# Six load slots for three, and the shift grids cleared by GpSimd, in a four-stage convolution and attention kernel

## The reference

```python
x = x + _L0_conv_ref(_gn(x), ...)   # shifted-window attention, 8 heads, windows of 8x8 at stride 2, then a projection
x = x + _L1_conv_ref(_gn(x), ...)   # grouped 3x3 convolution (32 groups), batch norm over all pixels, relu
x = x + _L2_conv_ref(_gn(x), ...)   # 1x1, 3x3 and 1x1 convolutions, each scanned over channel blocks, A + x
x = x + _L3_conv_ref(_gn(x), ...)   # the same with other weights
```

## Time and profile before

| | us |
|---|---|
| median of three runs | 2324.82 (2323.87 to 2324.83) |
| the profiled execution | 2317.36 |
| its span, first to last instruction | 2315.6 |
| first transpose to last statistics of the load | 5.2 to 75.7 |
| start of the tail stage | 1278.4 |
| first product of the strips | 1320.3 |

### The profile page before, as it was taken

One profiled execution on the slowest core, in us unless ns is written; L12 is line 12 of the kernel. 1 busy time (PEld: TensorE's weight loads), 2 busy tenths in 40 slices (PEclk: granted clock), 3 DMA queues, 4 the chain that ended last, 5 costly groups with the idle time before them and its releaser, 6 DMA issues. The chain is left out here.

```text
span 2315.6 us, 72190 instructions
## 1 busy us (share of the span) xinstructions
PE 2016.2 (87%) x29330; PEld 1068.7 (46%) x29330; DVE 1700.2 (73%) x3482; ACT 1150.2 (50%) x2577; POOL 1060.1 (46%) x1228
## 2 busy tenths in 40 slices
PE   5699889997999799986999279888999999999996
PEld 5455555554555455543566023333444433333332
DVE  5698999899888989893333788887776665566653
ACT  5576666765666566662223345444443433333330
POOL 0477777776777677765910364332222211111100
PEclk9899999999999999997999599999999999999997
DMA  7211101111111011101444777775444443444444
GB/s 269 85 37 37 49 34 36 50 36 47 36 50 36 33 50 36 51 33 57 103 102 104 273 268 228 212 238 160 128 130 141 139 119 101 122 123 125 123 102 110
DMA packets 225593, 243.72 MB, mean 105 GB/s; under 512 B 125680, under 2 KB 192496, under 8 KB 225264
## 3 DMA queue, kind: packets, MB, share of 16 engines
q1 hardware_dynamic: 225264, 239.10, 34.4%
HBM read 92.45 MB, written 89.65 MB: 79 GB/s over the span
## 5 line engine op out<-in xcount | busy, mean ns | idle before, releaser
L1235 POOL TENSOR_SCALAR l_x<-l_x,l_scale,l_shift 128x384 f32<-128x384 f32 x192 | 149.9, 781 | 597.0 <-PE banks L1653 590.5
L423 POOL TENSOR_TENSOR at_prob<-at_prob,at_inv 128x512 f32<-128x512 f32 x288 | 294.2, 1042 | 116.7 <-DVE at_inv L561 111.5
L488 ACT ACTIVATE at_prob<-at_prob 128x512 f32<-128x512 f32 x288 | 182.0, 632 | 306.8 <-DVE at_prob L551 306.7
L1611 PE MATMUL banks<-l_a,l_taps 128*32 128x384 f32 x3456 | 313.1, 493 | 19.6 <-ACT l_r L1307 19.6
L1626 PE MATMUL banks<-l_above,l_taps 128*32 128x384 f32 x1728 | 307.4, 489 | 4.5 <-issue 3.7
L1626 PE MATMUL banks<-l_below,l_taps 128*32 128x384 f32 x1728 | 306.1, 489 | 0.0
L1318 ACT ACTIVATE l_above<-l_below 96x384 f32<-96x384 f32 x144 | 75.5, 524 | 438.2 <-DVE l_below L1497 225.9
L601 PE MATMUL banks<-at_xn,at_w 128*64 128x256 f32 x2336 | 287.6, 389 | 3.2 <-ACT at_xn L440 3.2
L1483 DVE COPY l_old<-l_a 32x384 f32<-32x384 f32 x576 | 242.7, 421 | 11.4
L640 PE MATMUL banks<-const,at_prob 128*128 128x128 f32 x1152 | 184.6, 287 | 52.3 <-POOL at_prob L423 50.9
L404 POOL TENSOR_TENSOR at_turn<-at_turn,at_tables 128x256 f32<-128x256 f32 x292 | 215.4, 759 | 1.7 <-ACT at_turn L459 1.7
(11 more groups left out here) (162 smaller groups left out, 3555.0 us busy)
## 6 DMA issues: line engine op xcount, KB each, us to landing
l_x<-both SPq DMA_DIRECT2D x48, 768.0 KB, 4.5
l_rows<-l_r SPq DMA_DIRECT2D x768, 48.0 KB, 2.0
l_work<-both SPq DMA_DIRECT2D x36, 768.0 KB, 5.6
at_k_bd<-at_k SPq DMA_DIRECT2D x584, 32.0 KB, 1.8
load_raw<-in_x SPq DMA_DIRECT2D x36, 512.0 KB, 4.4
both<-l_x SPq DMA_DIRECT2D x24, 768.0 KB, 3.8
out<-l_x SPq DMA_DIRECT2D x24, 768.0 KB, 4.5
both<-x_res SPq DMA_DIRECT2D x20, 768.0 KB, 3.5
```

The source lines that it names most:

```text
L423: nc.gpsimd.tensor_tensor(prob[i][p][:, :, :], prob[i][p][:, :, :], inv[i][p][:, :].unsqueeze(2).broadcast_to([P, HEADS, WIN]), ALU.mult). ...
L488: nc.scalar.activation(prob[j % 2][p][:, :, :], prob[j % 2][p][:, :, :], ACT.Exp).then_inc(s["exped"], 1)
L1611: last = nc.tensor.matmul(grid(acc(k)[block_rows(c), :]), e[kind_of(k)][:, dy + 1, dx, :], a[:, k % A_RING, rows_, dx:dx + SIDE], start=(d ...
```

## The change

The load of x goes through six slots in place of three. The seven memsets of the grids leave VectorE, where they stood behind the first norm, and go to GpSimd, behind the memset of `a` and ahead of its first units. The semaphore `grids_zeroed` is then raised by GpSimd, and VectorE's wait for it stays where it was.

```diff
--- before.py
+++ after.py
@@ -151,7 +151,7 @@
 
 
 LOAD_T = 8
-LOAD_RING = 3
+LOAD_RING = 6
 LOAD_SPAN = LOAD_T * P
 
 
@@ -1213,6 +1213,10 @@
         def _(pool):
             nc.gpsimd.memset(a[:], 0.0).then_inc(s["a_zeroed"], 1)
             pool.wait_ge(s["a_zeroed"], 1)
+            for i in range(3):
+                nc.gpsimd.memset(above[i][:], 0.0)
+                nc.gpsimd.memset(below[i][:], 0.0)
+            nc.gpsimd.memset(zero[:, :], 0.0).then_inc(s["grids_zeroed"], 1)
             for n in range(FIRST_UNITS):
                 if first_by_pool(n):
                     pool.wait_ge(first_in[n // 2], 16)
@@ -1447,10 +1451,6 @@
             norm_c(0)
             norm_d(0)
             norm_e(0)
-            for i in range(3):
-                nc.vector.memset(above[i][:], 0.0)
-                nc.vector.memset(below[i][:], 0.0)
-            nc.vector.memset(zero[:, :], 0.0).then_inc(s["grids_zeroed"], 1)
             dve.wait_ge(s["grids_zeroed"], 1)
             dve.wait_ge(s["a_zeroed"], 1)
```

## The result

Median of six runs 2294.26 us (2289.18 to 2298.01) against 2324.82 us before (2323.45 to 2326.91): ratio 0.9868, 95% interval 0.9855 to 0.9882, 30.6 us or 1.3% faster. The profiled execution took 2292.79 us, span 2291.0.

The account below looks back on a forecast made before the run. TensorE bounds the late tail; the load is bound by too short a ring, the first strips by VectorE's grid clearing. 20.1 + 4.4 = 24.5 us off the median 2324.82 gives 2300.3 us; range 2294.5 to 2312.5.

Parts of the forecast that it names:

- Sum 55.6 against 75.74 now: Load of x: last statistics done at 55.6 us where the profiled execution had 75.74, so 20.1 us won.
- one low stretch of the clock: Load of x: 2.1 us added to the new load's end for one stretch at TensorE's lower clock.
- The pace of the new load: Load of x: VectorE's two statistics would be next late, at 1.29 us a span; DMA's lower price was 1.26.
- The grids leave VectorE: Tail stage, first strips: seven memsets gone from VectorE, tile 4 copied earlier, 4.4 us won (ends 0 and 7.3).
- Unit 4's load: Tail stage: issued 6.2 us earlier, after unit 0's store lands in 3.6 us; TensorE's product for tile 4 next late.
- The grids arrive on GpSimd: Tail stage: seven memsets, 6.7 us in sum, end before GpSimd's first add and cost nothing.
- cover: Tail stage: time between the end of GpSimd's memsets and its first add, forecast at 1.3 us.
- The port: Tail stage: memsets on GpSimd hold no small VectorE operation, cost 0; rival taking all 6.7 us, chance 0.04.
- The sum: Whole kernel: 20.1 us from the load plus 4.4 from the grids, 24.5 us won.
- DMA did not stay at 337 GB/s: Rival, load: DMA stays the bound at 337 GB/s, 17.3 us won in all, 2307.5 us; chance 0.19.
- the clock did not hold the load back: Rival, load: whole load at TensorE's low-clock pace, 1.79 us a span, 4.7 us won, 2315.7 us; chance 0.05.
- sharing among six transfers did not delay the first span: Rival, load: first span lands with the sixth, 5.8 us later, no later gain, 2326.2 us; chance 0.04.

Follow-up runs that it names:

- e1: The kernel before, unchanged (three slots, grids cleared by VectorE), run again: median 2324.27 us, ratio to before 0.9994.
- e3: The kernel after with three slots in place of six, grids still cleared by GpSimd: median 2320.53 us, ratio to before 0.9975.
- e2: The kernel before with six slots in place of three, grids still cleared by VectorE: median 2304.27 us, ratio to before 0.9908.
- e4: The kernel after, unchanged (six slots, grids cleared by GpSimd), run again: median 2298.05 us, ratio to before 0.9877.
- e7: The kernel after with the load's bn_stats over only the first half of each 512 columns: 2294.22 us, one run.
- e11: The kernel after with GpSimd clearing the grids twice, both sets behind the memset of a: median 2298.28 us, ratio to before 0.9898.
- e8: The kernel after with GpSimd clearing the grids before a, not behind it: median 2296.47 us, ratio to before 0.9887.

## Why the prediction was wrong, and where right

**The term that failed** is the load's "Sum 55.6 against 75.74 now". The new end was right (55.4); the old one was a single execution's, and the load of three slots is the very part that scatters: 75.7, 79.1 and 82.5 us in three executions, mean 79.1. The mean gain of the load is 79.5 - 56.0 = 23.5 us and not 20.1 (aggregates, three and four executions), so the term was 3.4 us too small, of the 6.1 by which the forecast missed the median. I had the warning in hand, since the profiled execution lay 7.5 us below the median, and had priced one low stretch of the clock at 2.1 us, but put it on the new load, where none came, and not on the old, where they were. The range was built on the same 75.74, so its lower end lacked these 3 to 7 us.

This is as far as the runs carry. The mean of three is itself rough, since the profiled executions of e1 and e3 were the longest of their twelve runs, and the median of e2, 21.5 us won (18.4 to 24.4), fits 20.1 as well as 23.5. Nor is the load all that scatters. The six runs of the kernel after lie 8.8 us apart, though its load ended within 0.9 us in five profiled executions, and the stretch between load and tail stage differs by 5 us with the same code. The other 2.7 us of the miss are of that size and stay open. That the result fell just outside the range and not just inside is chance: e4's median, 2298.05, lies inside.

**The pace of the new load**: right in size (1.28 for 1.29) by luck, wrong in cause. I named VectorE; e7 shows DMA, which happens to need the same time. The right sum hides two errors that cancel: no low stretch (+2.1 forecast), but 35 spans took 47.35 us, 2.2 more than at 1.29, through the first spans and a few gaps (1.32 us before 29.30).

**The grids leave VectorE**: 4.4 us forecast; 4.36 us at tile 4, 4.1 and 4.5 at the fold, 5.3 between the medians (0.25% by the ratio, interval 0.13 to 0.36%). Unit 4's load moved 7.5 us nearer, not 6.2, since unit 0 was stored in less than 3.6 us, and TensorE's product bounds it as said.

**The grids arrive on GpSimd**: 1.08 us a memset, cover of 1.3 forecast and 1.54 found, cost nothing; e11 shows the price once the cover is gone, 3.1 us at the first product for 4.8 us of delay.

**The port**: nothing, as taken from the rows. The Trainium skill (SBUF - State Buffer, Who interferes with whom) counts `tensor_scalar` among the operations that can take the shared port pair, and would then let it wait; with one column it took 0.15 us beside a memset, as beside an add in the earlier trace rows. That the four-column copy waits for the memset that GpSimd runs, the trace and e8 show with 1.86 and 0.47 us.

**The sum**: load 23.5 and grids 4.3 make 27.8. The two comparisons gave 30.6 and 28.6; what is left, 2.8 and 0.8 us, is within the scatter of single executions.

The rivals: none came. DMA did not stay at 337 GB/s, the clock did not hold the load back, and sharing among six transfers did not delay the first span (first product at 4.96, 5.22 before).

## What to carry to other kernels

Where an engine waits for landings while the DMA queue waits for that engine, count the slots: add them until the DMA share reaches 1 while transfers are queued (here 1.00 with five slots), and expect no more after that, whatever the landing time does. Before subtracting a new time from an old one, take the old stage from several executions, above all where the granted clock differs from one to the next; the distance of the profiled execution from the median is the warning. An initialisation can be moved to an engine with idle time at no cost only as long as it ends before that engine's first real work, and its worth is read at the first thing that was queued behind it.

## What the runs showed of the hardware that I had not expected

- TensorE's granted clock fell from its full level to half (2.4 to 1.2 GHz; 0.50 from 30 to 35 us of the kernel before) for stretches in every load of three slots (means 0.93, 0.87, 0.84) and in that of four (0.94), where TensorE often waits 0.5 us or more for a span to land. Before the first fall in the kernel before, its longest such wait behind the first landing was 1.7 us. The clock fell in none with five or more, where most waits are 0.2 us, and in neither where extra transposes filled the time (1.00 and 0.99).
- The end of the load scatters with it: three slots ended 6.8 us apart in three executions, six slots 0.9 us apart in five.
- The step between four slots and five: 66.4 to 55.8 us at the load's end and 8.4 us by the ratios (0.9928 to 0.9892), and nothing clear of the intervals from five to nine.
